# A one-column write by GpSimd, and a wait for it, behind each gather of neighbour rows in a graph layer

## The reference, cut to what matters

```python
messages = edge_val[:, None] * embeddings[edge_src]
neighbor_emb = jax.ops.segment_sum(messages, edge_dst, num_segments=embeddings.shape[0])
interaction_emb = neighbor_emb * embeddings
side_emb = (neighbor_emb + interaction_emb) @ W2.T + b2
```

## Time and profile before

| what | us |
|---|---|
| median of 2 runs (3125.46 to 3130.92) | 3128.19 |
| the profiled execution's own time | 3135.3 |
| its span, from the first to the last instruction | 3133.6 |
| busy: PE / DVE / ACT / POOL | 2220.0 / 1773.9 / 1038.1 / 2107.4 |
| first gather's start (L542) to the last one's end | 120.15 to 2249.80 |

### The profile page before, as it was taken

The page is one execution under the profiler, slowest core; times in us unless marked ns, Lnnn a source line. Parts: engine busy times, 40 slices in busy tenths (PEclk is TensorE's granted clock), DMA queues, the critical chain, the costliest instruction groups (busy, mean ns, idle before and its releaser), DMA issues.

```text
span 3133.6 us, 40481 instructions
## 1 busy us (share of the span) xinstructions
PE 2220.0 (71%) x12708; PEld 1672.6 (53%) x12708; DVE 1773.9 (57%) x4468; ACT 1038.1 (33%) x2247; POOL 2107.4 (67%) x1981
## 2 busy tenths in 40 slices
PE   0177777775666676767666565655559999999997
PEld 0044444443455554555544344433448888888887
DVE  7666666662445555556544343434376666666665
ACT  2122222220333333434322221222224445544453
POOL 2377777777777777777777777777535655565553
PEclk9999999996888888878877676778769999999999
DMA  7655555544455555555544444444432223332320
GB/s 250 212 146 153 150 146 150 149 137 122 144 154 154 154 157 155 158 150 159 152 138 137 129 136 133 134 134 134 111 97 56 34 55 72 64 69 44 69 35 9
DMA packets 270413, 386.94 MB, mean 123 GB/s; under 512 B 51528, under 2 KB 209998, under 8 KB 270096
## 3 DMA queue, kind: packets, MB, share of 16 engines
q0 software_dynamic: 105984, 245.21, 30.2%
q1 hardware_dynamic: 123346, 100.70, 10.4%
q10 hardware_dynamic: 40870, 38.41, 3.6%
HBM read 321.97 MB, written 67.21 MB: 124 GB/s over the span
## 4 chain that ended last, share of the span: by engine, by line
POOL 46%; PE 21%; issue 19%; DVE 8%; DMA 4%; ACT 2%; DVEq 0%; ACTq 0%; POOLq 0%; SPq 0%
POOL rows_sb L542 45%; PE bank L775 5%; PE bank L777 5%; PE bank L776 5%; PE bank L619 3%; DMA rows_sb<-xn_scratch,src_sb 2%; DVE rows_sb L1223 1%; DVE rows_sb L1215 1%; DMA arena<-x_in 1%; ACT rows_sb L1396 1%; DVE rows_sb L1209 1%; DMA xn_scratch<-arena 1%; DVE rows_sb L1225 1%; PE bank L785 1%; PE bank L649 1%
## 5 line engine op out<-in xcount | busy, mean ns | idle before, releaser
L542 POOL DMA_INDIRECT rows_sb<-xn_scratch,src_sb x1664 | 1622.7, 975 | 595.8 <-issue 589.4
L619 PE MATMUL bank<-rows_sb,s_sb 128*48 128x256 f32 x3328 | 544.6, 483 | 599.3 <-DMA rows_sb<-xn_scratch,src_sb 583.7
L619 PEld LDWEIGHTS bank<-rows_sb,s_sb 128*48 128x48 f32 x3328 | 275.8, 151 | 790.2 <-issue 675.5
L580 POOL DMA_INDIRECT out_dram<-rows_sb,sca_i x128 | 222.4, 1737 | 307.1 <-DVE rows_sb L1228 277.9
L1293 ACT COPY sums<-bank 112x256 f32<-112x256 f32 x208 | 77.4, 372 | 1050.9 <-PE bank L619 1050.9
L965 DVE TENSOR_TENSOR acc<-acc,bank 128x96 f32 x416 | 105.9, 255 | 369.0 <-DVE acc L965 163.2
L775 PE MATMUL bank<-w_lo,hid 128*128 128x256 f32 (+1 forms) x1024 | 292.2, 285 | 0.0
L777 PE MATMUL bank<-w_hi,hid 128*128 128x256 f32 (+1 forms) x1024 | 289.4, 283 | 0.0
L776 PE MATMUL bank<-w_hi,hid 128*128 128x256 f32 (+1 forms) x1024 | 289.4, 283 | 0.0
L1060 DVE TENSOR_TENSOR arena<-bank,gateb_sb 128x8 f32<-128x8 f32 x98 | 16.1, 164 | 387.5 <-PE bank L724 387.3
L775 PE MATMUL bank<-xg_hl,w_hi 128*128 128x512 f32 (+1 forms) x512 | 210.4, 411 | 28.4 <-ACT relu L1387 27.4
(11 more groups left out here) (186 smaller groups left out, 4553.4 us busy)
## 6 DMA issues: line engine op xcount, KB each, us to landing
rows_sb<-xn_scratch,src_sb POOLq DMA_INDIRECT x1664
arena<-xn_scratch SPq DMA_DIRECT2D x194, 128.0 KB, 3.0
w_raw<-ffn_w_in SPq DMA_DIRECT2D x16, 1024.0 KB, 6.5
xnt_scratch<-arena SPq DMA_DIRECT2D x97, 128.0 KB, 2.1
arena<-xnt_scratch SPq DMA_DIRECT2D x97, 128.0 KB, 2.4
arena<-x_in SPq DMA_DIRECT2D x97, 128.0 KB
h_scratch<-arena ACTq DMA_DIRECT2D x97, 128.0 KB
out_dram<-arena ACTq DMA_DIRECT2D x97, 128.0 KB
```

Of the source, the lines that this page charges most:

```text
L542: pool.indirect_dma_start(out=rows_sb[:, c % ROW_SLOTS, :], out_offset=None, in_=xn_d, in_offset=bass.IndirectOffsetOnAxis(ap=src_sb[:, c: ...
L580: pool.indirect_dma_start(out=out, out_offset=bass.IndirectOffsetOnAxis(ap=sca_i[0:r, col:col + 1], axis=0), in_=yo[0:r, q % YS, i, :], in ...
L619: m = pe.matmul(psum[p % 2][i * HALF:i * HALF + WIN, 0:D], s_sb[:, p % S_SLOTS, i * GROUP + j, :], rows_sb[:, c % ROW_SLOTS, :], start=j = ...
```

## The change

Behind every gather of L542, GpSimd writes zeros to the column `flag_f` and adds one to `pool_seq`, and then waits until `pool_seq` has counted this write. The wait stands ahead of the next gather, and for a group's first gather ahead of the wait at L540.

```diff
                         out=rows_sb[:, c % ROW_SLOTS, :], out_offset=None, in_=xn_d,
                         in_offset=bass.IndirectOffsetOnAxis(ap=src_sb[:, c:c + 1], axis=0)
                     ).then_inc(row_ld[g % len(row_ld)], 16)
+                    pool.memset(flag_f[:, :], 0.0).then_inc(pool_seq, 1)
+                    pool.wait_ge(pool_seq, c + 1)
```

## The result

The changed kernel takes 3303.24 us (median of 2 runs, 3300.66 to 3305.82) against 3128.19: a ratio of 1.0553, with a 95% interval of 1.0525 to 1.058. The forecast was 3301.

The account below looks back on a forecast made before the run. POOL's 1.28 us beat over 1664 gathers was taken as the bound; write 0.10, restart 0.27, longer gather 0.03, less the gap's 0.30, added 166 us to 3135.3: 3301 us. Its own range was 3230 to 3380, the wider one 3150 to 3450.

Parts of the forecast that it names:

- The bound: Gather stage, L542: POOL's time per gather, 1.280 us, sets the pace; anything added is multiplied by 1664.
- The sum: Per gather beat: 0.10 + 0.27 + 0.03 - 0.30 = 0.10 us more, times 1664 gives 166 us.
- the experts' first gather: Expert stage's first gather, released by VectorE's L1163, started 0.27 us later; taken as the restart after the write.
- the 0.08 in front of a whole gap: Alternative restart: release after 0.08 us, as for POOL's subtraction behind its cast, then the full 0.30: 0.38.
- the scatter's 0.88: Accumulating scatter started 0.88 us after its release by L1228; not taken, upper end 0.68 per beat, 4267 us.
- The 0.03 for a longer gather: Gather of L542: 0.98 us after idle time against 0.95 after a gather; 0.03 charged to every gather.
- The old gap: POOL's idle time between consecutive gathers of L542 before the change, subtracted from each beat as 0.30 us.
- The held-up write: Writes slowed beside VectorE's L954 and L956: 0.03 us per beat, 51 us, 3352 us; left out of the sum.
- Rival (a): Between gathers: write hidden in the gap, not slower, 0 to 50 us, 3135 to 3185; chance 0.14.
- Rival (b): Between gathers: write's 0.10, release 0.08, then whole 0.30 again; 0.18 per beat, 300 us, 3435; chance 0.18.
- Rival (c): Gather start: nothing prepared while waiting, so 0.88 us after release as for the scatter; 4267 us; chance 0.05.
- Rival (d): Gather stage: PE becomes the bound as its clock falls to 0.50; 265 us more, 3400; chance 0.04.

Follow-up runs that it names:

- thin_before: Kernel before, with PE multiplying only the first of each group's four chunks, all gathers kept: 3120.07 us.
- thin_after: Changed kernel, with PE multiplying only the first of each group's four chunks, all gathers kept: 3299.87 us.
- thin_no_wait: Changed kernel with an unwaited write to used-up row-number columns, PE multiplying only the first of each group's four chunks: 3118.67 us.
- two_rounds: Changed kernel with two writes, each waited for, behind each gather: 3699.32 us, 1.0692 of the kernel before.
- late_wait: Changed kernel, writing to used-up row-number columns and waiting only for the previous beat's write: 3542.41 us, 1.024 of the kernel before; repeated on another chip, 1.0256.
- wide: Changed kernel with the write 128 columns wide, to used-up row numbers, waited for, behind all but the first 152 gathers: 3504.01 us, 1.0129 of the kernel before.
- no_wait: Changed kernel with the write going to used-up row-number columns and no wait: 3477.08 us, 1.0045 of the kernel before; repeated on another chip, 1.0028.
- thin_late_wait: Changed kernel waiting only for the previous beat's write, to used-up columns, PE multiplying only the first of each group's four chunks: 3124.12 us.

## Why the prediction was right, point by point

**The bound** was right: POOL's beat between gathers times 1664, nothing moved behind the stage, and PE only waited longer.

**The sum** came out at 0.10 us per beat, and 165.6 / 1664 = 0.0995 was measured, but not all of its terms. The write was taken at 0.10 and took 0.115. The start of the next gather was taken at 0.27 after its release and took 0.27: the experts' first gather was the right row, and neither the 0.08 in front of a whole gap nor the scatter's 0.88 was. The 0.03 for a longer gather was too much: 979 ns against 975 is 0.004, and between thin_before and thin_after it is 0.017 (965 and 982); a usual gather behind a write takes the same 0.94 to 0.95, not the 0.98 of the one after idle time. In its place came two costs which together have its size: 0.015 more for the write, and 1.36 / 96 = 0.014 for the long stretch at every 96th gather, which no row of before could show. The old gap, taken at 0.30, was 0.305, which takes back 0.005. The working's 166 us against 165.4 between the profiled executions is owed to this cancelling, which is luck; the mechanism, a write and behind it a restart of 0.27, was right. Against the 175 between the medians it is 9 us short, and against the 180 of the thin runs 14; with single executions 5 to 10 us apart, the runs cannot tell how much of that is real. That 3301 lies 2 us from the measured 3303 is luck once more: it starts from an execution 7.1 us above the median.

**The held-up write** was rightly left out: the writes' mean is 115 ns and their median 113, so the 51 us reckoned for writes beside L954 and L956 did not come. Counted in the trace of the changed kernel, 173 writes run beside one of these two products; their mean is 113 ns, and none is above 115. It is the gathers that are longer there, 1040 ns in the mean for the 314 beside a product against 965 for the others. The Trainium skill, "SBUF — State Buffer", section "Who interferes with whom", by which a VectorE instruction with two SBUF inputs does not get in the way of a GpSimd instruction that only writes, agrees with what the writes show.

**Rival (a)** was wrong for this change and would have been right for another: a write that nobody waits for does vanish in the gap (thin_no_wait), so the 0.30 us does hold room beside the gather's preparation. What I held against it, that the wait is for the write's end, is what decided. In the rows of after, the 0.27 counts from the write's end as the trace reports it; this fits the Trainium skill, "Perfetto Trace Analysis", section "GPSIMD Engine Instruction", by which that end is the acknowledged write that raises the semaphore.

**Rival (b)** was not it: the gap is 0.38 and not 0.48. **Rival (c)** did not come in the changed kernel, though starts later than 0.27 exist: 0.60 in two_rounds and 0.72 in late_wait, where a gather has two semaphores to wait for. **Rival (d)** did not come on the first chip, where POOL's waits for PE in the changed kernel are 6.2 us in all; on two others PE holds POOL up in the kernel before already, not for the change, and there it hides part of it.

## What to carry to other kernels

Where one engine's beat sets a stage, a wait for its own instruction costs that instruction's length and the restart of what stands behind; the same instruction without a binding wait, or with the wait one beat later, can cost nothing. Where another engine holds it up, that does not carry over: there the late wait took 65 and 78 us more than no wait. Price a restart by a row in which the same kind of instruction was released by a semaphore, not by its gap in a running series. And measure such a change where the engine is the bound: on a chip where another engine held it up, the same 5.5% read as 1.7%.

## What the runs showed of the hardware that was not expected

- Every 96th gather starts 1.36 us later than the others when each gather waits for the write just ahead of it (17 times in the changed kernel, in thin_after and in two_rounds alike, and 16 times in wide, where the first of the places lies ahead of the first write). It does not show in before, no_wait, thin_before, thin_no_wait and thin_late_wait. In late_wait it shows at 10 of the 17 places, with gaps of 1.77 us behind a gather that was held up, so a wait that is met early does not always hide it. What happens there was not found; the number of instructions is not it.
- An indirect DMA started 0.24 us after the mark of PE's release with one semaphore to wait for, and 0.72 us with two. In two_rounds it was 0.60 although the other one had long been met, and in the changed kernel, where a group's first gather has two as well, 0.27.
- The kernel before took 3128 us in the first measurement, and 3461, 3423 and 3127 us on the three chips of the experiments. On the two chips with the longer times a result of PE reached ScalarE 23 and 25 us after the end of PE's rows. Why was not found.
